# Expert routing by groups of tiles inside the second attention, and expert 0's and 1's weights split ahead

## Chip, cores and metric

One core of a Trainium2 chip. The metric is device microseconds (us) of one execution. Engines: TensorE (PE, weight loads PEld), VectorE (DVE), ScalarE (ACT), GpSimd (POOL); SyncE (SP) only issues transfers.

## The reference, cut to what matters

x is 8 sequences of 512 rows of 512 values, which is 4096 tokens; two layers follow each other:

```
x = x + xattn0(layernorm(x), ctx, mask)      # 16 heads of 32, 77 keys
x = x + ffn0(layernorm(x))                   # 8-bit x, ternary w, depthwise conv, silu
x = x + xattn1(layernorm(x), ctx)            # 16 heads of 64
x = x + moe(layernorm(x))
# moe: logits = x @ router (8 experts); the two best; softmax over the two
#      for each expert e over its tokens: out += w * ((silu(x@w13[e][:, :1024]) * (x@w13[e][:, 1024:])) @ w2[e])
```

## The kernel before, in words

The program is a chain of blocks; all engines meet between two of them: `context`, `attention0`, `ffn`, `attention1`, `routing`, `experts`, `combine` (`program`, L2083 on). A tile is 128 tokens, so there are 32 (NT), four to a sequence (TPS). x stays in SBUF. Products that need more than bf16 are made of a high and a low bf16 part, three products in place of one (PRODUCTS).

**attention0** runs a software pipeline of 35 steps. In step s PE does the scores of tile s (`score_half`, twice), the mix of tile s-2, the turn of tile s+1, the output product of tile s-3 and four flips of tile s-1. Both halves of the scores begin with two bf16 products that write the mask's bias into PSUM (L423); the score products add to it. DVE takes the maximum over PSUM (`shift`, L552), subtracts it into the SBUF buffer `e` (L556), sums after ACT's exponential (L565) and inverts; POOL multiplies by the inverse (L397) and adds the output bias (L400). PE may overwrite a half's scores once DVE has subtracted. Turns, flips and mixes share a ring of three PSUM banks in the fixed order of `unit`. At tile 8, POOL also issues one transfer (L392) that fills all of `sorted_x` in DRAM with zeros: 9216 rows of 2 KB.

**ffn** runs nine iterations over the sequences. In each, POOL multiplies 16 chunks (L1124, after ACT's row of scales L1336) and adds 16 (L1135); ACT's silu and rounding wait for POOL chunk by chunk, through four buffers. DVE is the busiest engine.

**attention1** is the same sort of pipeline. In every four steps, two turn two tiles of the next sequence each (`turns`) and two project the next sequence's queries (`projections`, 48 products of 512 columns each step). Units of the three-bank ring are freed by ACT's copy (`unit_copied`) or by DVE's low part (`unit_low`); `place` fixes their order. The output product of a tile is 24 products (L790). SP loads keys and values per sequence.

**routing** normalizes all 32 tiles (DVE L1677), turns them (PE L1605), and makes logits for groups of four tiles with the router as the stationary operand (L1585, then turned back, L1594). DVE then takes one chain of small operations over all tiles at once (L1685 to L1749): the two best experts, counts, a prefix sum over tiles, a region of `sorted_x` for each expert that begins where the last one's ends, rounded up to 128 rows, and the row of every token in it. Only then each tile is normalized again (L1755), split into high and low (ACT L1657, DVE L1763) and scattered by two indirect DMAs on POOL's queue (L1567). Between these tiles ACT and DVE split the weights of experts 0 and 1, 24 chunks of 128x1024 (L1636, L1669), into `plan.weights13` and `plan.weights2`.

**experts** goes over 72 slots of 128 rows (SLOTS, L1467); each does the products of one expert, whose number PE reads from `plan.expert`. SP loads slot rows from `sorted_x` (L1897, L1902) and stores results to `sorted_y`. POOL splits the weights of experts 2 to 7 as places come free (L1881, L1883). **combine** gathers two rows for each token from `sorted_y` (L2058) and adds them to x.

Of the kernel before, what the change touches and what calls it, by code (L numbers as in the profile page):

```python
# [27 lines left out]
P = 128  # L28
B, S, D = 8, 512, 512
KEYS = 77  # L30
H = 16
# [282 lines left out]
def attention0(nc, core, keys, values, w):  # L314
# [6 lines left out]
    FILL_AT = 8  # L321
    with ExitStack() as stack:
# [15 lines left out]
        zero_row = sb("zero_row", [P, 2 * D], BF16)  # L338
# [8 lines left out]
        scores_ready = sem("scores_ready"); topped = sem("topped"); shifted = sem("shifted")  # L347
# [3 lines left out]
        row_zeroed = sem("row_zeroed"); cleared = sem("cleared")  # L351
        block = stack.enter_context(nc.Block("attention0"))

# [30 lines left out]

        @block.gpsimd
        def _(pool):
            nc.gpsimd.memset(zero_row[:, :], 0.0).then_inc(row_zeroed, 1)
            pool.wait_ge(bo_in, 16)
            for t in range(NT):
                if t == FILL_AT:  # L390
                    pool.wait_ge(row_zeroed, 1)
                    pool.dma_start(w["sorted_x"].rearrange("(s p) d -> p s d", p=P),  # L392
                                   zero_row[:, :].unsqueeze(1).broadcast_to([P, SLOTS, 2 * D])).then_inc(cleared, 16)
# [7 lines left out]
            pool.wait_ge(cleared, 16)  # L401

        @block.tensor
        def _(pe):
# [13 lines left out]
            def score_half(t, half):  # L418
                b = t // TPS
                if t >= 1:  # L420
                    pe.wait_ge(shifted, 2 * (t - 1) + half + 1)
                for g in range(2):
                    nc.tensor.matmul(scores[half][:, g, 0:QUARTER], core.ident_bf[:, :],  # L423
                                     bias[:, t, :].unsqueeze(1).broadcast_to([P, CH, KEYS]), start=True, stop=False)
                for c in range(CH):
                    for g in range(2):
# [3 lines left out]
                                                start=False, stop=(c == CH - 1))  # L430
# [32 lines left out]
            for step in range(NT + 3):  # L463
                if step < NT:
                    pe.wait_ge(unit_copied, unit["turn", step] + 1)
                    pe.wait_ge(bias_made, step // TPS + 1)
                    for half in range(2):
                        score_half(step, half)
# [13 lines left out]
        def _(act):  # L482
# [42 lines left out]
            for step in range(NT + 2):  # L525
# [10 lines left out]
                if 1 <= step <= NT:  # L536
                    for q in range(ROWS_OF):
                        flipped(step - 1, q)

        @block.vector  # L540
        def _(dve):
# [6 lines left out]
            def shift(t, half):  # L548
                raw = scores[half][:, :, 0:QUARTER].rearrange("p g (h k) -> p g h k", h=CH)
                tops = top[:, half, :].rearrange("p (g h) -> p g h", g=2)  # L550
                dve.wait_ge(scores_ready, 2 * t + half + 1)
                nc.vector.tensor_reduce(tops, raw, AX.X, ALU.max).then_inc(topped, 1)  # L552
                dve.wait_ge(topped, 2 * t + half + 1)
                if t >= 2:
                    dve.wait_ge(unit_ready, unit["flip", t - 2, 2 * half + 1] + 1)
                nc.vector.tensor_tensor(grouped(e[:, t % 2, half, :]), raw,  # L556
                                        tops.unsqueeze(3).broadcast_to([P, 2, CH, KEYS]), ALU.subtract
                                        ).then_inc(shifted, 1)
# [33 lines left out]
def attention1(nc, core, w):  # L592
# [7 lines left out]
    WIDTH = PER * KEYS  # L600
    with ExitStack() as stack:
# [5 lines left out]
        xn_t = sb("xn_t", [P, 2, KD, S], BF16)  # L607
        query = [sb(f"query{i}", [P, 2, CH, S], BF16) for i in range(2)]
        keys = sb("keys", [P, 2, 2, CH, KEYS], BF16)
        values = sb("values", [KEYS, 2, CH * P])  # L610
# [3 lines left out]
        probs_t = sb("probs_t", [P, 2, H, P])  # L614
        mixed_t = sb("mixed_t", [P, 2, 2, CH, P], BF16)
        wq = sb("wq", [P, 2, KD, CH * P], BF16)
        wo = sb("wo", [P, 2, CH, D], BF16)
        bq = sb("bq", [P, CH])


        raw_q = probs_t[:, :, :, :].rearrange("p t h n -> p (t h n)").rearrange("p (k n) -> p k n", k=KD)
        raw_o = query[1][:, :, :, :].rearrange("p a c n -> p (a c n)").bitcast(F32).rearrange(
            "p (k n) -> p k n", n=D)
# [15 lines left out]
        out_ready = sem("out_ready"); out_added = sem("out_added"); stats_made = sem("stats_made")  # L639
# [831 lines left out]
def routing(nc, core, plan, w, sorted_x):  # L1471

    E = EXPERTS
# [669 lines left out]
```

## Time and profile before

| | |
|---|---|
| three runs | 3048.58, 3050.35, 3052.56 us; median 3050.35 |
| profiled execution, its own time | 3052.12 us |
| its span in the trace | 3050.3 us |
| granted PE clock, mean | 0.919 |
| PE busy | 2499.0 us, 82% |

A line of the timeline has start and length in us, engine, line of the kernel, operation, result and operands, how many, and in brackets the idle time of the engine before it with what ended it. A group's line ends with busy us, mean ns of one, and idle us before. Busy time excludes waits, except that an operation held up after it began shows as a longer one.

### The profile page before, as it was taken

The numbers are of one execution on the slowest core, as the hardware profiler recorded it, in microseconds if no ns is written. First come the engines' busy times: TensorE is split into PE (matmuls) and PEld (weight loads), VectorE is DVE, ScalarE is ACT, GpSimd is POOL, SyncE is SP. The second block draws the span as 40 slices with busy tenths as digits, with TensorE's granted clock in tenths as the row PEclk, the third lists the DMA queues.
The fourth block names the chain that finished last, engine by engine and source line by source line (L and its number), as shares of the span: only waits on it lengthen the run. The fifth ranks groups of instructions, "written<-read, shape, count | busy, mean of one in ns | idle before, by whom it ended". The sixth has DMA issues, their size and how long they took to land. (4 is left out here: it accounts for less than half of the span.)

```text
span 3050.3 us, 46845 instructions
## 1 busy us (share of the span) xinstructions
PE 2499.0 (82%) x16388; PEld 1340.7 (44%) x16603; DVE 1610.2 (53%) x2256; ACT 1083.4 (36%) x1736; POOL 971.9 (32%) x803
## 2 busy tenths in 40 slices
PE   8899964566656699999980299999999999999960
PEld 5566632222222355565640144444444444444430
DVE  4566668899897556566656322232333323332225
ACT  2355535788876444444342211111111111111110
POOL 0243312677768111111105400050643406320027
PEclk9799986798988799999995699999999999999985
DMA  6350010000000200000035301030322303220128
GB/s 229 116 214 36 2 56 0 1 1 1 0 1 0 72 10 14 10 14 10 1 97 171 143 28 34 28 117 28 117 82 77 100 30 114 72 62 28 34 74 274
DMA packets 88750, 190.29 MB, mean 62 GB/s; under 512 B 25189, under 2 KB 28261, under 8 KB 88117
## 3 DMA queue, kind: packets, MB, share of 16 engines
q1 hardware_dynamic: 63269, 98.43, 9.9%
q0 software_dynamic: 25360, 90.21, 8.9%
q8 instruction: 81, 1.33, 0.2%
q14 instruction: 40, 0.33, 0.0%
HBM read 120.65 MB, written 67.96 MB: 62 GB/s over the span
## 5 line engine op out<-in xcount | busy, mean ns | idle before, releaser
L1926 PE MATMUL e_gate_up<-weights,e_x_t 128*128 x3314 | 758.0, 380 | 9.2 <-ACT e_x_t L1980 1.8
L1926 PEld LDWEIGHTS e_gate_up<-weights,e_x_t 128*128 128x128 bf16 x3456 | 332.7, 98 | 376.9 <-issue 4.3
L2013 DVE TENSOR_TENSOR e_mid<-e_gate,e_gate_up 128x512 f32<-128x512 f32 x144 | 99.1, 688 | 644.7 <-ACT e_gate L1986 644.7
L1946 PE MATMUL e_out<-weights,e_mid_t 128*128 x1726 | 384.6, 379 | 1.2 <-DVE e_mid_t L2026 1.1
L1986 ACT ACTIVATE e_gate<-e_gate_up 128x512 f32<-128x512 f32 x144 | 86.1, 598 | 682.4 <-PE e_gate_up L1926 682.4
L1946 PEld LDWEIGHTS e_out<-weights,e_mid_t 128*128 128x128 bf16 x1728 | 169.1, 98 | 204.8 <-issue 1.2
L1205 PE MATMUL f_out<-f_w,hidden 128*128 128x512 f16 x512 | 141.3, 402 | 102.6 <-ACT hidden L1307 101.9
L708 POOL TENSOR_TENSOR a_e<-a_e,a_total 128x616 f32<-128x616 f32 x64 | 76.5, 1217 | 452.4 <-DVE a_total L960 452.4
L1135 POOL TENSOR_TENSOR f_shared<-f_shared 128x512 f32<-128x512 f32 x128 | 181.2, 1416 | 122.4 <-DVE f_shared L1413 122.4
L1876 POOL TENSOR_TENSOR e_token<-e_token 1x1 f32<-1x1 f32 x6 | 1.1, 184 | 657.5 <-PE e_out L1946 657.5
L1124 POOL TENSOR_TENSOR hidden<-hidden,f_up_row 128x512 f32<-128x512 f32 x128 | 178.6, 1406 | 86.6 <-ACT f_up_row L1336 86.6
L2026 DVE COPY e_mid_t<-e_mid_flip 128x1024 bf16<-128x1024 bf16 x144 | 98.9, 688 | 181.7 <-PE e_mid_flip L1936 181.7
L736 PE MATMUL a_ring<-a_xn_t,a_wq 128*128 128x512 bf16 x752 | 169.1, 382 | 7.8 <-issue 7.0
L790 PE MATMUL a_out<-a_wo,a_mixed_t 128*128 128x512 bf16 x737 | 164.3, 379 | 4.5 <-issue 3.0
L1184 PE MATMUL f_product<-f_xq_t,f_w 128*128 128x512 bf16 x489 | 140.0, 413 | 30.3 <-DVE f_padded L1381 18.5
L1992 ACT ACTIVATE e_y_rows<-e_out 128x512 f32<-128x512 f32 x72 | 43.0, 597 | 340.2 <-PE e_out L1946 340.2
L1413 DVE SCALAR_TENSOR_TENSOR f_shared<-f_padded,f_conv_w,f_shared 128x512 f32<-128x512 f32 x128 | 152.1, 1189 | 14.6 <-ACT f_shared L1290 14.3
L2058 POOL DMA_INDIRECT o_y<-sorted_y,plan_rows x64 | 68.8, 1075 | 284.6 <-PEq L2044 265.4
L1883 POOL TENSOR_TENSOR weights<-raw_weights,weights 128x1024 bf16<-128x1024 f32 x72 | 154.0, 2140 | 6.1
L397 POOL TENSOR_TENSOR a_e<-a_e,a_total 128x616 f32<-128x616 f32 x64 | 76.5, 1217 | 196.1 <-DVE a_total L567 196.1
L1916 PE MATMUL e_flip<-ident_bf,e_x_rows 128*128 128x128 bf16 x576 | 44.3, 220 | 114.5 <-DMA e_x_rows<-sorted_x 114.5
L2019 DVE TENSOR_TENSOR e_mid_parts<-e_mid,e_mid_parts 128x512 bf16<-128x512 f32 x144 | 130.3, 905 | 5.0
(236 smaller groups left out, 4134.0 us busy)
## 6 DMA issues: line engine op xcount, KB each, us to landing
raw_weights<-in_w POOLq DMA_DIRECT2D x72, 512.0 KB, 3.9
sorted_x<-a_zero_row POOLq DMA_DIRECT2D x1, 18432.0 KB, 57.0
e_x_rows<-sorted_x SPq DMA_DIRECT2D x72, 256.0 KB, 2.7
sorted_y<-e_y_rows SPq DMA_DIRECT2D x72, 256.0 KB, 2.0
raw_weights<-in_w SPq DMA_DIRECT2D x24, 512.0 KB, 3.7
x<-in_x SPq DMA_DIRECT2D x4, 2048.0 KB, 20.1
out<-x SPq DMA_DIRECT2D x32, 256.0 KB
hidden<-in_w_t SPq DMA_DIRECT2D x1, 4096.0 KB, 17.4
```

Source lines behind the costliest of these rows:

```text
L736: last = nc.tensor.matmul(bank(u)[:, :], wq[:, a, k, c * P:(c + 1) * P], xn_t[:, d, k, :], start=(k == 0 and a == d == 0), stop=(k == KD - ...
L790: last = nc.tensor.matmul(out[:, :], mixed_t[:, t % 2, a, c, :], wo[:, d, c, :], start=(c == 0 and a == d == 0), stop=(c == CH - 1 and (a, ...
L1124: nc.gpsimd.tensor_tensor(hidden[:, j, :], hidden[:, j, :], up2_row[:, :], ALU.mult).then_inc(scaled_up, 1)
L1135: nc.gpsimd.tensor_tensor(y[:, j % BUF, :], y[:, j % BUF, :], side[:, j % BUF, :], ALU.add).then_inc(right_added, 1)
L1184: last = nc.tensor.matmul(product[j % 2][:, :], w1[:, k, j % HC * P:(j % HC + 1) * P], xq_t[:, parity, k, :], start=(k == 0), stop=(k == K ...
L1205: last = nc.tensor.matmul(out[i][:, :], hq[:, j, i * P:(i + 1) * P], w2[:, j, :], start=False, stop=(j == HC - 1))
L1413: nc.vector.scalar_tensor_tensor(y[:, j % BUF, :], padded[:, j % BUF, 0:S], conv_w[:, j, 0:1], y[:, j % BUF, :], ALU.mult, ALU.add).then_i ...
L1883: nc.gpsimd.tensor_tensor(parts[1], plan.raw[:, n % 2, :], parts[0], ALU.subtract).then_inc(split, 1)
L1926: last = nc.tensor.matmul(gate_up[half][:, part, :], x_t[:, u, a, k, :], plan.weights13[:, bass.ds(expert % 2, 1), b, k, col:col + 512], s ...
L1946: last = nc.tensor.matmul(out[:, :], mid_t[:, a, j, :], plan.weights2[:, bass.ds(expert % 2, 1), b, j, :], start=(j == 0 and a == b == 0), ...
L2013: nc.vector.tensor_tensor(mid[:, half, :], gate[:, half, :], gate_up[half][:, 1, :], ALU.mult).then_inc(mid_made, 1)
L2019: nc.vector.tensor_tensor(mid_parts[:, half, 1, :], mid[:, half, :], mid_parts[:, half, 0, :], ALU.subtract).then_inc(mid_low, 1)
```

## The change

1. **Routing moves into attention1**, in nine groups of tiles: seven of four, then two of two. A group's small statistics (`moments`, `norms`; an ACT square root between exponentials), the logits (`logits_of`, tokens as the stationary operand, 8 columns), the choice (`choose`) and the rows (`counts`, `rows_of`) take places at fixed steps behind the tiles: pairs are turned again at the group's last tile + 5 and + 6, the choice and the rows follow one and two steps on. The pipeline has 39 steps in place of 35. The units `route`, `logits` and `counts` join the three-bank ring.
2. **Each expert gets a region of 4096 rows** of `sorted_x` (33792 rows with a margin), so that a group's rows are known without the counts of later tiles. POOL splits (`split`) and scatters (`scatter`) group by group. `slots_and_weights`, once at the end, works out which slot starts where (`plan.base`) and the rows in `sorted_y` (`plan.y_rows`). SP reads a slot's start from SBUF before its load.
3. **The zero fill moves** from attention0 to ffn's iteration 1, ahead of POOL's wait there, and is four transfers of 8448 rows.
4. **Experts 0 and 1**: their 24 chunks are loaded and split in attention0 (steps 4 to 27, high part on ACT, low part on POOL), stored to DRAM as bf16, and loaded in attention1 by SP: expert 0 during its last steps, w13 of expert 1 after the last output product, w2 of expert 1 after the last scatter has landed.
5. **The mask in attention0** is added by DVE while it moves the scores from PSUM into `e`; maximum and subtraction then work in SBUF. The bias products on PE go. PE may overwrite a half's scores after that addition.
6. **71 slots** in place of 72.
7. attention1's large buffers are laid over the expert weights' places.

```diff
-                for g in range(2):
-                    nc.tensor.matmul(scores[half][:, g, 0:QUARTER], core.ident_bf[:, :],
-                                     bias[:, t, :].unsqueeze(1).broadcast_to([P, CH, KEYS]), start=True, stop=False)
...
+                nc.vector.tensor_tensor(grouped(now), raw, bias[:, t, :].unsqueeze(1).unsqueeze(1).broadcast_to(
+                    [P, 2, CH, KEYS]), ALU.add).then_inc(biased, 1)
+                nc.vector.tensor_reduce(top[:, half, :], heads(now), AX.X, ALU.max).then_inc(topped, 1)
+                nc.vector.tensor_tensor(heads(now), heads(now), top[:, half, :].unsqueeze(2).broadcast_to(
+                    [P, HALF, KEYS]), ALU.subtract).then_inc(shifted, 1)
...
+                n = t - SPLIT_AT                        # POOL, attention0
+                if 0 <= n < len(early):
+                    pool.wait_ge(high_made, n + 1)
+                    nc.gpsimd.tensor_tensor(parts[:, n % 2, 1, :], raw[:, n % 2, :], parts[:, n % 2, 0, :],
+                                            ALU.subtract).then_inc(low_made, 1)
...
+                if isinstance(b, int) and b == 1:       # POOL, ffn
+                    blocks = ROWS // P // FILLS
+                    for f in range(FILLS):
+                        part = w["sorted_x"][f * blocks * P:(f + 1) * blocks * P, :]
+                        pool.dma_start(part.rearrange("(s p) d -> p s d", p=P),
+                                       zero_row[:, :].unsqueeze(1).broadcast_to([P, blocks, 2 * D])
+                                       ).then_inc(w["cleared"], 16)
                 if has_back:
                     pool.wait_ge(row2_copied, b)
...
+            def logits_of(t):
+                for i in range(2):
+                    for k in range(KD):
+                        last = nc.tensor.matmul(bank(u)[:, i * E:(i + 1) * E], row_t[:, i, k, :], router[:, k, :],
+                                                start=(k == 0), stop=(k == KD - 1))
...
+                for t in route_turns(step):             # POOL, attention1
+                    split(t)
+                if step in rows_at:
+                    g = rows_at[step]
+                    pool.wait_ge(rows_made, g + 1)
+                    for t in GROUPS[g]:
+                        scatter(t)
...
+            sp.wait_ge(out_ready, NT)                   # SP, attention1
+            for a in range(2):
+                sp.dma_start(plan.weights13[:, 1, a, :, :], w["split13"][1, a].rearrange("(k p) n -> p k n", p=P)
+                             ).then_inc(plan.early_in[1], 16)
+            sp.wait_ge(late_out, 32 * SENT)
+            for a in range(2):
+                sp.dma_start(plan.weights2[:, 1, a, :, :], w["split2"][1, a].rearrange("(k p) n -> p k n", p=P)
+                             ).then_inc(plan.early_in[1], 16)
...
+SLOTS = (2 * B * S) // P + EXPERTS - 1
+REGION = B * S
+FILLS = 4
+ROWS = EXPERTS * REGION + 1024
```

## Rows read from the trace of the kernel before

**Rows 1.** The page's head: the span

```profile
span 3050.3 us, 46845 instructions
```

**Rows 2.** Busy time of each engine by stage: stretch, length, PE, PEld, DVE, ACT, POOL

```profile
core 0: us, PE busy (x) PEld busy (x) DVE busy (x) ACT busy (x) POOL busy (x), PEclk, DMA share, GB/s
98.00:435.00 337.00, 320.35 (x3072) 221.28 (x3072) 213.52 (x348) 165.64 (x293) 119.88 (x105) 0.95 0.22 80
435.00:1003.00 568.00, 324.38 (x1341) 137.75 (x1364) 490.53 (x476) 398.70 (x626) 353.27 (x256) 0.83 0.02 7
1003.00:1547.00 544.00, 508.58 (x4689) 307.56 (x4736) 318.90 (x500) 236.37 (x395) 76.54 (x64) 0.97 0.07 18
1547.00:1730.00 183.00, 52.44 (x232) 25.04 (x233) 99.80 (x193) 66.40 (x100) 73.62 (x73) 0.65 0.48 164
1730.00:2951.00 1221.00, 1210.18 (x6767) 604.14 (x6908) 396.53 (x576) 197.45 (x289) 275.19 (x226) 1.00 0.19 61
```

**Rows 3.** Timeline of the routing stage: its two ends

```profile
1546.98 0.69 DVE L964 TENSOR_TENSOR x<-x,a_out 128x512 f32<-128x512 f32 x1 [4.79 <-PE a_out L790]
...
1718.46 0.97 POOL L1567 DMA_INDIRECT sorted_x<-r_xn_t,plan_rows  x1 [0.30 <-issue]
...
1727.01 0.82 SPq L1897 DMA_DIRECT2D e_x_rows<-sorted_x  x2
...
1729.66 1.04 PE L1916 MATMUL e_flip<-ident_bf,e_x_rows 128*128 128x128 bf16 x8 [114.47 <-DMA e_x_rows<-sorted_x]
```

**Rows 4.** Timeline of attention0: one step of a tile

```profile
250.18 0.80 DVE L552 TENSOR_REDUCE a_top<-a_scores 128x8 f32<-128x616 f32 x1 [1.68 <-PE a_scores L428]
...
258.27 0.43 PE L423 MATMUL a_scores<-a_bias,ident_bf 128*128 128x308 bf16 x2
...
258.63 1.12 PE L428 MATMUL a_scores<-keys,a_xn_t 32*128 32x77 f32 x16
...
259.79 0.80 DVE L552 TENSOR_REDUCE a_top<-a_scores 128x8 f32<-128x616 f32 x1 [1.68 <-PE a_scores L428]
```

**Rows 5.** Groups by line: what attention0 runs, and the weight splitting

```profile
L556 DVE TENSOR_TENSOR a_e<-a_scores,a_top 128x616 f32<-128x616 f32 x64 | 51.2, 800 | 2.2
...
L565 DVE TENSOR_REDUCE a_total<-a_e 128x8 f32<-128x616 f32 x64 | 50.7, 792 | 16.8 <-ACT a_e L502 15.1
...
L397 POOL TENSOR_TENSOR a_e<-a_e,a_total 128x616 f32<-128x616 f32 x64 | 76.5, 1217 | 196.1 <-DVE a_total L567 196.1
...
L400 POOL TENSOR_TENSOR x<-x,a_bo 128x512 f32<-128x512 f32 x32 | 40.7, 1271 | 0.0
...
L1636 ACT ACTIVATE weights<-raw_weights 128x1024 bf16<-128x1024 f32 x24 | 25.1, 1045 | 0.8 <-DMA raw_weights<-in_w 0.8
...
L1883 POOL TENSOR_TENSOR weights<-raw_weights,weights 128x1024 bf16<-128x1024 f32 x72 | 154.0, 2140 | 6.1
```

**Rows 6.** Tile e_mid_parts: least, median and longest ns of one subtraction

```profile
L2019 DVE TENSOR_TENSOR e_mid_parts<-e_mid,e_mid_parts x144: 691/693/2501, 1741.4 to 2939.9; 128x512 bf16<-128x512 f32 x144
```

**Rows 7.** Timeline of PE: two tiles turned; four logits tiles turned back

```profile
1230.39 1.34 PE L725 MATMUL a_ring<-ident,a_xn 128*128 128x128 f32 x8
...
1567.22 0.41 PE L1594 MATMUL r_logits_p<-ident,r_prefix 8*128 8x8 f32 x4
```

**Rows 8.** Groups by line, 1607:1626: one small DVE operation of routing

```profile
L1698 DVE TENSOR_TENSOR r_gap<-r_best 128x32 f32<-128x32 f32 x1 | 0.2, 192 | 0.0
```

**Rows 9.** Timeline of POOL: issue of the clearing transfer; idle before iteration 1

```profile
181.61 3.12 POOL L392 DMA_DIRECT2D sorted_x<-a_zero_row  x1
...
547.99 1.28 POOL L1124 TENSOR_TENSOR hidden<-hidden,f_up_row 128x512 f32<-128x512 f32 x1 [10.76 <-ACT f_up_row L1336]
```

**Rows 10.** DMA issues: KB each, us from issue to landing

```profile
sorted_x<-a_zero_row POOLq DMA_DIRECT2D x1, 18432.0 KB, 57.0
...
e_x_rows<-sorted_x SPq DMA_DIRECT2D x72, 256.0 KB, 2.7
...
a_probs_t<-in_wq_t SPq DMA_DIRECT2D x1, 2048.0 KB, 8.3
```

More of the change, by code:

```diff
@@ new lines, in attention1 @@
+        row_t = sb("row_t", [P, 2, KD, P])
+        sent = sb("sent", [P, SENT, 2, D], BF16)
+        before = sb("before", [P, P])
+        ones = sb("ones", [P, P])
+        order = sb("order", [P, E])
+        order_i = sb("order_i", [P, E], I32)
+        first_i = sb("first_i", [P, E], I32)
+        slot_i = sb("slot_i", [P, SLOTS], I32)
+        slot_f = sb("slot_f", [P, SLOTS])
+        norm_tmp = sb("norm_tmp2", [P, 5, TPS])
+        logits = sb("logits", [P, TPS, E])
+        mark = sb("mark", [P, TPS, E])
@@ new lines, in attention1 @@
+        rank = sb("rank", [P, TPS])
+        chosen = sb("chosen", [P, 2, TPS, E])
+        both = sb("both", [P, TPS, E])
+        run = sb("run", [P, TPS + 1, E])
+        upto = sb("upto", [P, E])
+        rows = sb("rows", [P, 2, NT])
+        best = sb("best", [P, 2, NT])
+        gap = sb("gap", [P, NT])
+        slots_of = sb("slots_of", [P, E])
+        ends = sb("ends", [P, 2, E])
+        slot_e = sb("slot_e", [1, 2, SLOTS])
+        first_f = sb("first_f", [P, E])
+        jump = sb("jump", [P, E])
@@ L711, in _ @@
+            for i in range(SENT):
+                pool.wait_ge(sent_out[i], 32 * LATE // SENT)
+            pool.wait_ge(late_out, 32 * SENT)
         @block.tensor
@@ L784, in output @@
             def output(t):
-                pe.wait_ge(unit_low, low[unit["mix", t, 1]] + 1)
+                pe.wait_ge(unit_low, low[unit["mix", t, 1]])
                 if t >= 1:
@@ L799, in _ @@
                 project(0, c)
-            for step in range(NT + 3):
+            for step in range(STEPS):
                 if step < NT:
@@ L815, in _ @@
                         flip(step - 1, q)
+                for t in route_turns(step):
+                    turn(("route", t))
                 for c in projections(step):
@@ L890, in _ @@
                                          ).then_inc(weights_high, 1)
-            norm(TPS)
-            norm(TPS + 1)
-            for step in range(NT + 2):
-                if step >= 2:
+            norm(("turn", TPS))
+            norm(("turn", TPS + 1))
+            for step in range(STEPS):
+                if 2 <= step < NT + 2:
                     mixed(step - 2, 0)
```

748 lines of the change are left out of this document (387 added, 361 removed).

## The prediction

> **What bounds the kernel now.** The forecast is against the profiled execution, 3052.1 us (span 3050.3, about 1.8 around it [rows 1]); the median of the three runs shown is 1.7 lower. I read the windows by stage first, then the timeline at the seams, then groups and DMA issues. By stage, PE is busy 320 of 337 us in attention0, 509 of 544 in attention1 and 1210 of 1221 in experts: these three are PE's, at the full granted clock but for their first microseconds. ffn is DVE's (491 of 568), with POOL at 353 in series with it. The routing stage is nobody's: in 183 us PE does 52, DVE 100 [rows 2]. The timeline shows its length as a reader should measure it: the last output product is in at 1546.98 (DVE's addition starts), the first slot's turn starts at 1729.66, PE idle 114.5 us before it, and before that POOL issues the last scatter at 1718.46 and SP the first slot load at 1727.01 [rows 3]. So 182.7 us lie between the products of attention1 and those of experts.
>
> **1. That gap.** Nearly all of it goes, but a tail stays for the tiles that are late by nature. Counted from the last output product: addition, statistics and `moments` some 2.7 us; a small DVE operation takes 0.19 us [rows 8], 0.21 with its semaphore. `logits_copy` and 12 operations of `rows_of` for tiles 24 to 27 end at about 6.6; choice (13) and `norms` (6) for the last pairs at 10.4; turn, copy, logits, a second choice and the last rows at 21.5. POOL is behind that: from 6.6 on it has 8 scatters at 0.97 + 0.30 = 1.27 us [rows 3], two splits of 1.7 (half of 1.05 and 2.14, the 1024-column price [rows 5]), then 4 and 4 scatters: 6.6 + 10.2 + 3.4 + 5.1 + 5.1 = 30.4. The last scatter before was followed by 7.6 us until the block was over [rows 3]: 38. Then comes an ordering cost: SP issues w2 of expert 1, 2 MB, when the scatters have landed, and the first slot's rows stand behind it in the same queue: 8.3 us as a 2 MB load [rows 10], then 2.7 [rows 10]: about 49. `slots_and_weights` (some 35 small operations, 10 us) runs beside the scatters. So 182.7 - 49.5 = **-133**; bounds -148 (no queueing, quicker landing) and -118 (cold PE, slower transfers).
>
> **2. PE in attention1.** PE is the bound there, so what it gets is paid. Two tiles' turns take 1.34 us: 0.67 each [rows 7]. Logits are four products per tile that stream only 8 columns; between four small ones with 8 rows of weights, 0.41, and a few with cold clock, 1.1 [rows 7], I take the turns' 0.67, since both load four full 128x128 fp32 weights. 28 tiles x 1.34 = 37.5 (the last four are in the tail). Counts: 7 x 0.5 = 3.5. A stall: where a logits unit follows two turns, the ring's bank is freed by DVE's low part of the second mix, which comes after the second `shift`, about 1.5 us after PE wants it, in 5 groups: 7.5. **+48**; bounds +32 and +65. The two table loads per group on ACT, the 25 to 30 small operations on DVE and POOL's splits and scatters I cost at nothing: ACT is busy 236 of 544, DVE 319, POOL 77 [rows 2], and the pipeline is two steps deep; without that cover they would be 9 x 2.6, 9 x 6 and 9 x 10 us.
>
> **3. 71 slots.** 1221 / 72 [rows 2]: **-17**, PE-bound, no doubt in it.
>
> **4. attention0.** A step takes 259.79 - 250.18 = 9.61 us with PE full; each bias pair delays the scores by 258.63 - 258.27 = 0.36 [rows 4], so PE would need 8.9. But DVE's shift grows from two passes to three of 0.80 [rows 5] per half, near 8.5 a step. And there is a collision. The new subtraction has both operands in SBUF; where POOL works on SBUF, such a subtraction took 0.69 at best and 2.50 at worst [rows 6], that is, it waited for POOL's 2.14 to end [rows 5]. POOL's order is multiply, multiply, bias, low part: from the end of the second subtraction it is 1.1 + 2 x 1.22 + 1.27 = 4.75 us until the low part starts [rows 5] (ACT's high part, 1.05 after its flips, is done at 4.65), and it holds to 6.9. The next tile's first subtraction is due at 5.3: it waits 1.6, and the loop through exponential, flip copies and scores closes at about 10.05. 24 steps x (10.05 - 9.61) = +10.6, the 8 without splitting x -0.7 = -5.6: **+5**; bounds -22 (no collision) and +20. DMA for the 24 chunks (0.5 MB in, 0.5 out per step) is hidden.
>
> **5. The zero fill in ffn.** Before, one fill of 9216 rows cost POOL 3.12 us to issue [rows 9], 57.0 to land [rows 10]. Now POOL issues four of 8448 rows at 2.9, in a place where it sat idle 10.76 us [rows 9]. If the queue takes them all, that is 11.5 against 10.8: +1, the lower bound. But what is issued has to be held somewhere until it has been moved, and no row of the trace shows more than those 9216 rows in flight; this asks for 33792 within 12 us, while one fill takes 57 to land. The upper bound is that each fill must wait until the one before has landed, 57.0 x 8448 / 9216 = 52.3: POOL is free again after 3 x 52.3 + 2.9 = 160 us, 149 later than before. What is queued behind it is `scale_up` and the addition of every chunk, and with four buffers everything in ffn waits after four chunks; some 6 us of DVE's work is done meanwhile. **+143**. Two full fills together (16896 rows) are 1.8 times the most that was seen in flight; I take the upper bound, since the only row of this kind is for a fill that had the queue to itself.
>
> The Trainium skill bears on this: "SBUF — State Buffer" (section "SBUF size: 192, 224, or 256?") sets aside 16 KiB a partition for POOL's descriptors, and "DMA: Bandwidth & Descriptors" (sections "Terms" and "SWDGE vs HWDGE vs iDMA") gives a descriptor 16 bytes and each direction 16 partitions. My estimate from these is 16384 rows in flight: two fills don't fit, by little. By that page alone the sum would be the upper bound if room is given back a whole transfer at a time. No row here shows a queue that is full.
>
> **Sum.** -133 + 48 - 17 + 5 + 143 = **+46**: 3052 + 46 = **3098 us**. combine and the rest of ffn are unchanged.
>
> **Rivals.**
> A. *The queue takes all four fills* (other side: faster). Place: POOL's queue at ffn's second iteration; it decides from the second fill on. For it: 9216 rows were taken in 3.1 us without a sign of waiting; against it: 3.7 times as much is asked for. -133 + 48 - 17 + 5 + 1 = -96: 2956, 2925 to 2990. Chance 0.25.
> B. *Room is given back row by row.* POOL then writes as fast as rows land: 33792 rows take 4 x 52.3 = 209 us; POOL is free when the last 9216 (57) are left, or with room for nearly twice as many, about 110: 152 to 110, less 10.8 and 6: +93 to +135. 3048 to 3090. Chance 0.13.
> C. *Fill by fill, as forecast.* 0.62; within it the collision in attention0 fails to happen in a third of cases, which gives 3072. Its own range is 3068 to 3125.
> That the change doesn't do what it says (fewer slots, less work between the stages) I see no way for.
>
> **How the numbers follow.** About 0.2% (6 us) can be told from no change. Slower: C but for 0.02, and most of B (0.07) = 0.67; faster: A, 0.02 of B and a remnant of C = 0.29; same 0.04. The likeliest is 3098. Range 2955 to 3125: C with its bounds, B, and the upper half of A; left out are the lower half of A (0.12) and C's edges. Cases of both signs hold weight, so C's own range above is the one to read if POOL's stall is there.
>
> **What would show it.** In the profile after: POOL idle or long issues at ffn's second iteration with about 52 us between fills, PE's granted clock at its low level there, and ffn some 140 us longer; if the four issues stand within 12 us, step 5 is wrong and A holds. attention0: the first half's subtraction with a mean of 2 us or more in steps 4 to 27 and steps of 10 us; steps of 8.9 would refute it. attention1: about 48 us longer to its last product, with turns and logits of 0.67 a tile; then 45 to 55 us to the first turn of experts, with the slot's load landing 10 us or more after its issue. A slot remains 17.0. If the gap is above 65 us, POOL's scatters were slower than 1.27; if attention1 grows by over 70, the ring or DVE, not PE's own work, bounds it.

## The result and the profile after

The changed kernel takes 3150.77 us (median of 4 runs, 3148.74 to 3156.01) against 3049.47: a ratio of 1.0335, 95% interval 1.0317 to 1.0353. Slower, as forecast, but by 101 us where 46 were forecast, and 26 us above the end of the range. The profiled execution spans 3154.2 us, 103.9 more than the one of before.

By stage, the windows of the kernel after (columns as in [rows 2]; the rows are attention0, ffn, attention1 to its last product, the gap, experts):

```profile
core 0: us, PE busy (x) PEld busy (x) DVE busy (x) ACT busy (x) POOL busy (x), PEclk, DMA share, GB/s
98.10:440.90 342.80, 305.71 (x2944) 211.88 (x2944) 278.73 (x405) 191.14 (x316) 166.82 (x121) 0.89 0.29 95
440.90:1162.30 721.40, 328.78 (x1341) 139.13 (x1364) 495.48 (x490) 400.53 (x629) 364.38 (x270) 0.76 0.28 102
1162.30:1803.50 641.20, 584.63 (x5050) 364.39 (x5099) 372.70 (x777) 290.01 (x474) 175.24 (x177) 0.92 0.14 45
1803.50:1845.00 41.50, 10.90 (x60) 9.84 (x58) 21.92 (x101) 5.51 (x9) 20.62 (x25) 0.55 0.70 260
1845.00:3055.00 1210.00, 1198.53 (x6674) 592.99 (x6816) 392.80 (x568) 195.82 (x284) 276.43 (x226) 1.00 0.19 62
```

| stage, us | before | after | difference | forecast |
|---|---|---|---|---|
| context | 96.6 | 98.1 | +1.5 | 0 |
| attention0 | 334.7 | 342.9 | +8.1 | +5 |
| ffn | 571.9 | 721.3 | +149.4 | +143 |
| attention1, to the last addition | 543.8 | 641.3 | +97.5 | +48 |
| gap, to the first turn of experts | 182.7 | 41.5 | -141.2 | -133 |
| experts | 1220.9 | 1210.0 | -10.9 | -17 |
| combine | 99.7 | 99.2 | -0.5 | 0 |

One term is off by more than 9 us: attention1, by 49.5 of the 58 that are missing. PE is busy 585 us there where it was 509, and the granted clock is 0.92 where it was 0.97 [rows 2]. At two levels of 1.0 and 0.5 (2.4 and 1.2 GHz), a mean of 0.92 means, as an estimate, 16% of 641 us, or 103 us, at the low level; before it was 6% of 544, or 33.

**ffn.** The timeline of POOL after, at ffn's iteration 1, answers to [rows 9]:

```profile
547.30 2.92 POOL L1487 DMA_DIRECT2D sorted_x<-f_zero_row  x1
598.48 2.85 POOL L1487 DMA_DIRECT2D sorted_x<-f_zero_row  x1 [48.26 <-issue]
649.55 2.82 POOL L1487 DMA_DIRECT2D sorted_x<-f_zero_row  x1 [48.22 <-issue]
700.58 2.83 POOL L1487 DMA_DIRECT2D sorted_x<-f_zero_row  x1 [48.20 <-issue]
703.43 3.71 POOL L1480 TENSOR_TENSOR hidden<-hidden,f_up_row 128x512 f32<-128x512 f32 x3
```

The four issues stand 51 us apart, each 2.9 us long, and POOL starts its first multiplication 156 us after the first issue, at 703.43. Before, it was idle for 10.8 us at this point.

**The gap.** The timeline from attention1's last addition to the first turn, which answers to [rows 3]:

```profile
1803.52 0.69 DVE L1187 TENSOR_TENSOR x<-x,a_out 128x512 f32<-128x512 f32 x1 [1.22 <-PE a_out L979]
...
1832.93 0.96 POOL L852 DMA_INDIRECT sorted_x<-weights,plan_rows  x1 [0.30 <-issue]
...
1835.62 0.98 SPq L821 DMA_DIRECT2D weights<-split  x2
...
1841.41 0.09 POOL L1926 MEMSET e_token<- 1x3 f32 x1 [7.53 <-POOLq L634]
...
1842.39 1.54 SPq L1978 DMA_DIRECT2D e_x_rows<-sorted_x  x2
...
1845.04 1.04 PE L1997 MATMUL e_flip<-ident_bf,e_x_rows 128*128 128x128 bf16 x8 [18.69 <-DMA e_x_rows<-sorted_x]
```

POOL's last scatter ends at 1833.9, 30.4 us after the addition began: the chain of 16 scatters and two splits came out to the tenth of a us in all. POOL is then held for 7.5 us as before, and 3.6 us later PE has its rows. w2 of expert 1 was issued at 1835.62, inside those 7.5 us.

**attention1.** The groups of PE's products in attention1 (a pair's logits are 8 products, which the trace shows as 16 records; before, all turns took 22.8 us, a pair of them 1.34 us [rows 7]; the last line is the output product in the kernel before):

```profile
L979 PE MATMUL a_out<-weights 128*128 128x512 bf16 x736 | 184.2, 412 | 4.4 <-issue 2.9 <-DVE weights L1161 0.3 <-DVE a_logits L1222 0.2
...
L891 PE MATMUL a_ring<-ident,a_xn 128*128 128x128 f32 x247 | 41.5, 309 | 17.3 <-ACT a_xn L1031 13.1 <-DVE weights L1161 3.7
...
L903 PE MATMUL a_ring<-a_router,a_row_t 128*128 128x8 f32 x224 | 32.5, 282 | 8.3 <-DVE weights L1161 7.5 <-ACT a_row_t L1039 0.7
```

```profile
L790 PE MATMUL a_out<-a_wo,a_mixed_t 128*128 128x512 bf16 x737 | 164.3, 379 | 4.5 <-issue 3.0 <-DVE x L964 0.9
```

The logits are 32.5 us, the turns 41.5, and the output product of 24 full-width matmuls, which the change leaves alone, takes 412 ns a record where it took 379, which adds some 20 us (184.2 against 164.3). What goes with it stands in the timeline of two steps (the first three lines, then the last three) and the windows beside the second:

```profile
1340.51 0.63 PE L891 MATMUL a_ring<-ident,a_xn 128*128 128x128 f32 x4 [1.25 <-DVE weights L1161]
1342.64 2.71 PE L903 MATMUL a_ring<-a_router,a_row_t 128*128 128x8 f32 x16 [1.51 <-DVE weights L1161]
1345.58 7.52 PE L979 MATMUL a_out<-weights 128*128 128x512 bf16 x23 [0.23 <-issue]
...
1356.80 1.97 PE L967 MATMUL a_ring<-weights,raw_weights 77*64 77x128 f32 x32
1358.70 1.95 PE L903 MATMUL a_ring<-a_router,a_row_t 128*128 128x8 f32 x16
1360.78 6.75 PE L979 MATMUL a_out<-weights 128*128 128x512 bf16 x23
```

```profile
1356.00:1360.00 4.00, 4.00 (x92) 3.77 (x86) 2.99 (x4) 2.27 (x5) 0.00 (x0) 1.00 0.01 4
1360.00:1364.00 4.00, 3.87 (x14) 1.82 (x15) 3.82 (x10) 0.72 (x1) 1.58 (x2) 0.58 0.00 0
```

At the full clock the logits take 1.95 us a pair, not 1.34. In the second step PE is idle for no more than 0.13 us before or after them, and yet the granted clock goes from 1.00 to 0.58 in the next 4 us: the output product takes 6.75 us where 5.13 is its length at the full clock. In the first step PE had waited 1.25 us ahead of the last turns and 1.51 us ahead of the logits, and the clock is at 0.50 from 1344 to 1350 (windows of 2 us); there the output product takes 7.52.

### The profile page after: what moved, and what is told of

Same layout as the page of the kernel before. It is cut to its first block and busy times, and to the rows that moved or that the text cites. A ratio compares the mean times of both kernels' runs of the same rounds, so it can differ in the third digit from the quotient of the medians.

```text
span 3154.2 us, 47443 instructions
## 1 busy us (share of the span) xinstructions
PE 2512.8 (80%) x16357; PEld 1363.7 (43%) x16571; DVE 1651.6 (52%) x2498; ACT 1101.0 (35%) x1744; POOL 1074.8 (34%) x895
## 5 line engine op out<-in xcount | busy, mean ns | idle before, releaser
L2007 PE MATMUL e_gate_up<-weights,e_x_t 128*128 x3268 | 748.0, 380 | 9.0 <-ACT e_x_t L2061 1.8
L2107 DVE COPY e_mid_t<-e_mid_flip 128x1024 bf16<-128x1024 bf16 x142 | 97.5, 687 | 180.9 <-PE e_mid_flip L2017 180.9
L1568 PEld LDWEIGHTS f_out<-f_w,hidden 128*128 128x128 f16 x512 | 42.7, 102 | 335.8 <-ACT hidden L1670 298.4
L979 PE MATMUL a_out<-weights 128*128 128x512 bf16 x736 | 184.2, 412 | 4.4 <-issue 2.9
L1744 DVE TENSOR_TENSOR f_padded<-f_product,f_down_row 128x512 f32<-128x512 f32 x128 | 87.6, 684 | 183.8 <-PE f_product L1547 176.0
L925 PE MATMUL a_ring<-weights 128*128 128x512 bf16 x752 | 169.5, 383 | 8.1 <-issue 7.3
L2139 POOL DMA_INDIRECT o_y<-sorted_y,plan_y_rows x64 | 67.7, 1058 | 268.6 <-PEq L2125 249.4
## 6 DMA issues: line engine op xcount, KB each, us to landing
sorted_x<-f_zero_row POOLq DMA_DIRECT2D x4, 16896.0 KB, 50.8
```

The costliest lines, as they stand in the source:

```text
L925: last = nc.tensor.matmul(bank(u)[:, :], wq[:, a, k, c * P:(c + 1) * P], xn_t[:, d, k, :], start=(k == 0 and a == d == 0), stop=(k == KD - ...
L979: last = nc.tensor.matmul(out[:, :], mixed_t[:, t % 2, a, c, :], wo[:, d, c, :], start=(c == 0 and a == d == 0), stop=(c == CH - 1 and (a, ...
L1568: last = nc.tensor.matmul(out[i][:, :], hq[:, j, i * P:(i + 1) * P], w2[:, j, :], start=False, stop=(j == HC - 1))
L2007: last = nc.tensor.matmul(gate_up[half][:, part, :], x_t[:, u, a, k, :], plan.weights13[:, bass.ds(expert % 2, 1), b, k, col:col + 512], s ...
L2139: pool.indirect_dma_start(out=y[:, t % BUFFERS, c, :], out_offset=None, in_=sorted_y, in_offset=bass.IndirectOffsetOnAxis(ap=plan.y_rows[: ...
```

## The experiments

### Where POOL's 150 us went: spread and eighths

`spread` issues the four fills in four iterations of ffn:

```diff
-                if isinstance(b, int) and b == 1:
+                fills = {0: (0,), 1: (1,), B - 2: (2,), B - 1: (3,)}
+                if isinstance(b, int) and b in fills:
                     blocks = ROWS // P // FILLS
-                    for f in range(FILLS):
+                    if b == 0:
+                        pool.wait_ge(w2_in, 16)
+                    for f in fills[b]:
```

> The changed kernel with its four fills issued in four different iterations of ffn (0, 1, 6, 7; the one in iteration 0 once ffn's second weights have landed) in place of all four in iteration 1. Theory: a fill of 8448 rows is taken by the queue at once when the one before has landed (51 us), so no issue waits; ffn falls from 721 to about 572 us and the kernel from 3151 to 3002 us (3000 to 3010). Rival (the fills cost ffn time by what they move, not by where POOL waits): each still costs some 20 us or more, 3030 to 3100 us.

Measured: 3010.35 us (3005.69 to 3012.63), 0.9853 of before (0.9835 to 0.9872). ffn takes 578.1 us in place of 721.3, 6 more than before. The fills move the same bytes; nearly all that they cost was POOL's wait. With this one edit the changed kernel takes 1.5% less than before, a small difference, but its interval leaves no change out.

`eighths` sets `FILLS = 8` with all eight at iteration 1.

> The changed kernel with eight fills of 4224 rows in place of four of 8448, all still at ffn's iteration 1. A fill of 4224 rows should land in 25.5 us. If the queue takes only one transfer at a time whatever its size, POOL waits for seven: 179 us, 3176 us. If it waits for room by rows and gives it back a transfer at a time, two in flight (8448 rows) give 153 us as now (3151 us) and three in flight (12672 rows) give 128 us: 3125 us.

Measured: one run of 3145.07 us, ffn 717.0. The timeline of POOL's issues in eighths (x3 are three issues one behind another):

```profile
543.47 5.55 POOL L1487 DMA_DIRECT2D sorted_x<-f_zero_row  x3
617.32 5.44 POOL L1487 DMA_DIRECT2D sorted_x<-f_zero_row  x3 [68.31 <-issue]
691.05 3.62 POOL L1487 DMA_DIRECT2D sorted_x<-f_zero_row  x2 [68.30 <-issue]
```

The times from issue to landing of the eight:

```profile
DMA to landing us min/median/max: 26.9/48.4/69.8
```

None of the three mechanisms came, although the time lies 6 us from the second number. Three fills, 12672 rows, were taken at once, so more than 8448 rows fit; but the fourth was not taken when the first had landed (the shortest landing is 26.9 us after its issue). It was taken 68 us after the third had been issued, when all three had landed (the longest landing is 69.8 us after its issue), and the seventh likewise after the next three. So POOL's queue, once an issue doesn't fit, waited until it was empty. That gives 3 + 3 + 2 and nearly the same wait as four single fills, 151 us from the first issue to the first multiplication against 156. The Trainium skill, "DMA: Bandwidth & Descriptors" (sections "Terms" and "SWDGE vs HWDGE vs iDMA") with "SBUF — State Buffer" (section "SBUF size: 192, 224, or 256?"), led to my estimate of 16384 rows in flight: the run agrees, as 12672 were taken and 16896 not.

### Why attention1 grew twice as much as forecast: wide, onek, behind, late

All four are edits of `spread`, whose attention1 takes 642.5 us:

```profile
1016.70:1659.20 642.50, 592.04 (x5099) 366.83 (x5100) 373.18 (x778) 290.30 (x474) 175.59 (x177) 0.91 0.14 45
```

`wide` streams 128 columns in each logits product and reads 8 of them:

```diff
-                        last = nc.tensor.matmul(bank(u)[:, i * E:(i + 1) * E], row_t[:, i, k, :], router[:, k, :],
+                        last = nc.tensor.matmul(bank(u)[:, i * 128:(i + 1) * 128], row_t[:, i, k, :],
+                                                router[:, k, :].unsqueeze(1).broadcast_to([P, 16, E]),
...
```

> The spread kernel with the logits products of attention1 streaming 128 columns (the router's 8 columns 16 times over) in place of 8; same number of products and weight loads, same logits. Theory T (the granted clock falls in and after the logits because PE streams almost nothing while it loads weights; this costs about 35 of the 97 us by which attention1 grew): the clock stays at 1.00 after the logits, the outputs behind them go back from 6.4 or 7.5 to 5.1 us, and the kernel is 20 to 35 us faster than spread, though 16 products of 128 columns take up to 0.3 us more a pair. Rival (the clock falls because PE stands idle at the ring's bank): no gain, or 4 us slower.

Measured: 2993.99 us (2989.30 to 2999.79), 0.980 of before; attention1 629.1 us, its granted clock 0.93 against 0.91. The output product behind one pair's logits, in spread and then in wide; both times PE had waited 1.51 us just before the logits:

```profile
1357.47 8.14 PE L979 MATMUL a_out<-weights 128*128 128x512 bf16 x24
```

```profile
1356.08 5.34 PE L980 MATMUL a_out<-weights 128*128 128x512 bf16 x24
```

So what theory T said of this place came: with 128 columns the clock stayed up behind most of the logits. The gain that it named (20 to 35 us) did not; the windows below say where the rest went.

`onek` keeps 2 of a pair's 8 logits products (k = 0 of each tile).

> The spread kernel with 2 of the 16 logits products per pair; it leaves out three quarters of the router's product and one accumulation, so the choice of experts is another one. It removes 14 products of 0.122 us at 14 of 16 pairs' places inside attention1: 24 us of PE by their price at full clock. Theory T: the clock's loss goes too, 45 to 60 us faster than spread in attention1. Rival (the clock has another cause): 24 us. The experts stage may differ a little, so attention1's own length is to be read.

(In this text 16 stands for the records of a pair; the kernel keeps 2 of 8 products.)

Measured: 2984.10 us (2980.89 to 2985.62); attention1 614.5 us, 28 less than spread. The three quarters of the 34.7 us that spread spends on logits are 26. So the removed work is nearly all of the gain (PE's busy time is 26.3 us less), and the clock stayed at 0.92. The 45 to 60 us of theory T did not come.

`behind` moves the logits and counts on PE behind the output product; nothing is removed:

```diff
-                if step - 1 in pairs_at:
-                    logits_of(pairs_at[step - 1])
-                if step in rows_at:
-                    counts(rows_at[step])
                 if step == 3:
                     pe.wait_ge(weights_low, 2 * KD)
                 if 3 <= step < NT + 3:
                     output(step - 3)
+                if step - 1 in pairs_at:
+                    logits_of(pairs_at[step - 1])
+                if step in rows_at:
+                    counts(rows_at[step])
```

> The spread kernel with PE doing the logits and the counts of a step behind that step's output product in place of ahead of it; the order of the ring's banks stays. Theory S (DVE's low parts of the mixes hold the ring's banks, 7.6 us of waits ahead of the logits, and small products back to back, mixes, turns and logits, bring the granted clock down): the waits ahead of the logits go (-7.6) and the output product of 23 full-width matmuls parts the small work, so that time at the low clock goes down from 112 us towards 50: attention1 15 to 35 us shorter. Rival (the clock answers to the total of small work in a stretch, whatever its order): -8 us, from the waits alone. Rival 2: DVE, which copies the logits ahead of its next work, now waits 5 us for them and hands it on: 0 or slower.

Measured: 2971.03 us (2969.95 to 2972.04), 0.9733 of before (0.9717 to 0.9749), 39 us faster than spread. Attention1's window and its groups:

```profile
1017.30:1619.90 602.60, 553.41 (x5067) 350.17 (x5115) 366.58 (x777) 291.69 (x476) 175.50 (x177) 0.97 0.15 50
```

```profile
1197.11 5.13 PE L979 MATMUL a_out<-weights 128*128 128x512 bf16 x23
1202.07 1.85 PE L903 MATMUL a_ring<-a_router,a_row_t 128*128 128x8 f32 x16
...
1209.81 5.13 PE L979 MATMUL a_out<-weights 128*128 128x512 bf16 x23 [0.16 <-issue]
```

```profile
L979 PE MATMUL a_out<-weights 128*128 128x512 bf16 x736 | 164.2, 379 | 4.9 <-issue 3.0 <-DVE x L1187 1.2
...
L891 PE MATMUL a_ring<-ident,a_xn 128*128 128x128 f32 x248 | 39.5, 295 | 19.8 <-ACT a_xn L1031 13.1 <-DVE weights L1161 6.3
...
L903 PE MATMUL a_ring<-a_router,a_row_t 128*128 128x8 f32 x235 | 27.3, 251 | 0.7 <-ACT a_row_t L1039 0.7
```

Attention1 is 39.9 us shorter than in spread, a little above the 15 to 35 that theory S named. PE's busy time is 38.7 us less, and its idle time (602.6 - 553.4 = 49.2, against 642.5 - 592.0 = 50.5) is the same within 1.3 (behind's trace lacks 32 of the 768 records of the output product and shows 3 us idle at them, spread's lacks none and shows 0, so the waits may have given up to 4 us of the gain): the waits ahead of the logits went, but others came at the turns and, behind the counts, at the flips. So the gain is in the main not the waits, as the first rival had it, but the clock: 0.97 in place of 0.91 is 36 us at the low level in place of 116, and 80 us at half speed are 40 us of lost work. The output product is back at 379 ns a record.

How the order does it is less plain than theory S had it. Logits stand in two steps of a group. In the first of them in the changed kernel, 12.7 us pass between two output products (1332.84 to 1345.58), waits of 1.25 and 1.51 us among them; in behind 8.4 us pass there (1188.75 to 1197.11). In the second step it is 7.8 us in the one and 7.7 in the other, with the same products in another order, and yet the next output product took 6.75 us in the changed kernel and 5.13 in behind.

`late` puts one memset on DVE ahead of attention1 in spread and changes nothing in its steps:

> The spread kernel with one memset of 2464 columns (some 2.6 us) on DVE at the start of attention1; nothing else in attention1 is changed. If the time lost to the low clock depends on how the steps fall against the chip's own rhythm, attention1 differs from spread's 642.5 by more than the 2.6 us put in (the same code took 619.9 to 642.5 in five kernels that reach it at different times), its time at the low clock differing from 112 us with it. If it depends on the code alone, 645.

Measured: one run of 2988.01 us. Its attention1 takes 618.4 us:

```profile
1017.30:1635.80 618.50, 571.22 (x5050) 356.26 (x5099) 373.79 (x779) 289.26 (x473) 174.75 (x172) 0.94 0.14 46
```

That is 24 us less than spread; the memset, 2.1 us long, stands ahead of this window. The whole kernel, by one run, takes 22 us less. PE's granted clock is 0.94. The same steps took 641.3 in the changed kernel, 642.5 in spread, 638.0 in eighths, 624.9 and 619.9 in mask_rows and nolow below. So attention1's time varies by up to 24 us among kernels whose steps are the same and that begin it at other times (one trace each), and the totals of `wide` and `onek` can't be judged against spread alone: 13 us of difference lie inside this band, and 28 are little more. A part of the band is a wait: PE waits for DVE ahead of its scores for 13.6 to 13.9 us in all in the changed kernel, spread and eighths, for 8.2 to 8.3 in the other three. With the logits behind the output product attention1 took 602.6, 602.5 and 602.7 us in three kernels (behind, quarters, lag), and 605.9 in `best`, which also had the wide logits: there the width brings nothing. Against the shortest stage in the old order the new order is 16 us shorter, against spread 40.

The place of the low clock tells more than its total. Windows of 1 us over attention1 give, as us at the low level (rounded, one trace each) by what stands where the fall begins:

| | in all | first 90 us | logits or the output product behind them | PE's wait ahead of the scores | last 40 us |
|---|---|---|---|---|---|
| before | 30 | 30 | - | 0 | 0 |
| spread | 111 | 36 | 51 | 10 | 14 |
| late | 76 | 35 | 37 | 0 | 3 |
| wide | 82 | 38 | 14 | 24 | 7 |
| onek | 95 | 34 | 20 | 27 | 14 |
| behind | 37 | 37 | 0 | 0 | 0 |

In the six kernels with the old order and the full logits of 8 columns, 37 to 51 us stand at the logits. With 128 columns it is 14 and with a quarter of the products 20, so the logits' own shape and number have a part in it; but both kernels lost 24 and 27 us behind waits of up to 2.2 us ahead of the scores, where spread lost 10. Behind the output product the logits cost none.

### attention0 and the gap: nolow, mask_rows, quarters, lag

The changed kernel's subtraction in attention0, by tile (least, median and longest ns):

```profile
L586 DVE TENSOR_TENSOR a_e<-a_e,a_top x64: 799/801/2162, 108.2 to 418.6; 128x616 f32<-128x616 f32 x64
```

`nolow` cuts POOL's low part to 8 columns (with the low halves cleared once ahead of the stage).

> The spread kernel with POOL's 24 low parts in attention0 cut to 8 columns each; it leaves out the low parts of the weights of experts 0 and 1 (they are zero). Theory (collision: DVE's subtraction inside SBUF waits for POOL's low part, and this sets the step): the longest subtraction falls from 2.16 to under 1.3 us, the step from 10.3 to about 9.0 to 9.6 us, attention0 from 341 to 300 to 320 us. Rival (DVE's third pass or PE's clock sets the step): 335 to 341 us.

Measured: one run of 2949.62 us. The same subtraction:

```profile
L588 DVE TENSOR_TENSOR a_e<-a_e,a_top x64: 799/800/802, 107.6 to 377.0; 128x616 f32<-128x616 f32 x64
```

The group's 64 subtractions take 51.2 us, 0.80 each, where they took 77.0 in the changed kernel. Attention0 takes 302.1 us, 39 less than spread, and its clock is 0.95 against 0.89. The collision was there, and it cost more than the forecast's 24 steps of 1.15, or 28 us. (`nolow` also takes the low parts' time off POOL; `quarters` below keeps it there.)

`mask_rows` restores the bias products on PE with maximum and subtraction from PSUM, and moves w2 of expert 1 behind the first rows:

```diff
-            sp.wait_ge(late_out, 32 * SENT)
-            for a in range(2):
-                sp.dma_start(plan.weights2[:, 1, a, :, :], ...
...
                 sp.dma_start(x_rows[:, s, :], x_rows_of(s)).then_inc(x_in[s], 16)
+            for a in range(2):
+                sp.dma_start(plan.weights2[:, 1, a, :, :], ...
```

> The spread kernel with two independent edits, read from their own stages: the mask's bias goes back to PE and the maximum and subtraction back to PSUM in attention0, and w2 of expert 1 is loaded behind the first two slots' rows. Attention0: if the collision of the third pass sets the step, it falls from 10.3 to 9.6 us (PE-bound, the clock stays at 1.00) and the stage from 341 to 335; if POOL's low part alone lengthens POOL's own chain enough, it stays at 341. Gap: the first turn comes 8 us earlier (41.6 to 33.5), by the 8.3 us of a 2 MB load; if x's rows were not queued behind it, nothing changes.

Measured: 2983.01 us (2977.73 to 2985.75). Attention0 takes 331.8 us (337.3 with the same edit in best) against 341.2: putting the mask on DVE cost 4 to 9 us here (attention0 differs by 5.5 us between these two kernels though its instructions are the same), beside POOL's low parts; without them (nolow) it gains 33 over before. The gap is 42.3 us against 41.6, so the order of the loads brings nothing:

```profile
1662.74 0.96 POOL L848 DMA_INDIRECT sorted_x<-weights,plan_rows  x1 [0.30 <-issue]
...
1671.23 0.09 POOL L1925 MEMSET e_token<- 1x3 f32 x1 [7.52 <-POOLq L634]
...
1672.21 1.53 SPq L1977 DMA_DIRECT2D e_x_rows<-sorted_x  x2
1673.78 1.06 SPq L1979 DMA_DIRECT2D weights<-split  x2
...
1674.87 1.03 PE L1999 MATMUL e_flip<-ident_bf,e_x_rows 128*128 128x128 bf16 x8 [18.72 <-DMA e_x_rows<-sorted_x]
```

The rows are issued ahead of w2 and yet the first turn comes as late. What holds it is the end of POOL's block, 7.5 us after the last scatter; w2 had passed in its shadow.

`quarters` is `behind` with each low part as four subtractions of 256 columns:

```diff
-                    nc.gpsimd.tensor_tensor(parts[:, n % 2, 1, :], raw[:, n % 2, :], parts[:, n % 2, 0, :],
-                                            ALU.subtract).then_inc(low_made, 1)
+                    for q in range(4):
+                        cut = slice(q * CW // 4, (q + 1) * CW // 4)
+                        low = nc.gpsimd.tensor_tensor(parts[:, n % 2, 1, cut], raw[:, n % 2, cut],
+                                                      parts[:, n % 2, 0, cut], ALU.subtract)
+                    low.then_inc(low_made, 1)
```

> The behind kernel with each of POOL's 24 low parts in attention0 as four subtractions of 256 columns in place of one of 1024. Collision theory: DVE's subtraction inside SBUF waits only for the piece that runs (about 0.55 us), so its longest falls from 2.16 to about 1.3 us and attention0 goes from 342 to 308 to 318 us; the kernel from 2971 to about 2941. Rival (POOL keeps the port through back-to-back instructions of its own): the subtraction still takes 2.2 us or more, 342 us.

The two operations in one step of behind, and then of quarters:

```profile
243.39 2.13 POOL L423 TENSOR_TENSOR a_parts<-a_raw,a_parts 128x1024 bf16<-128x1024 f32 x1
...
244.03 2.15 DVE L586 TENSOR_TENSOR a_e<-a_e,a_top 128x616 f32<-128x616 f32 x1
```

```profile
248.15 3.12 POOL L425 TENSOR_TENSOR a_parts<-a_raw,a_parts 128x256 bf16<-128x256 f32 x4
...
249.01 1.09 DVE L589 TENSOR_TENSOR a_e<-a_e,a_top 128x616 f32<-128x616 f32 x1
```

In behind, POOL's low part begins 0.6 us ahead of DVE's subtraction, which ends 0.66 us after POOL's does. In quarters the same subtraction takes 1.09 us (the longest of all 64 is 1.34), and POOL's four pieces take 3.12 together. Attention0 takes 310.4 us, and the kernel 2940.72 (2938.20 to 2943.77), 0.9632 of before (0.9615 to 0.9648): the fastest version of this study, 3.7% below the kernel before and 6.7% below the changed one. The Trainium skill, "SBUF — State Buffer" (section "Who interferes with whom"), has DVE and GpSimd share a pair of ports as an exclusive lock for the length of an instruction; this agrees, 2.15 us with one long piece and 1.09 with short ones.

`lag` is `behind` with the low part of a chunk a step later and ahead of POOL's bias addition.

> The behind kernel with POOL's low part of a chunk done a step later and ahead of the bias addition in place of behind it, so that it runs from 242.2 to 244.3 where it ran from 243.4 to 245.5 and DVE's subtraction is due at 244.0 (times of the step read in behind's trace). Collision theory: the subtraction waits 0.3 us at most, attention0 comes near the 302 us of nolow: 302 to 315; the kernel 2971 - 30 to 40 = 2931 to 2941. Rival (the addition of the bias, one SBUF operand pair too, now falls on the subtraction and holds it as long): 330 to 342 us.

Measured: 2956.07 us (2953.51 to 2958.23), 15 less than behind; attention0 326.0 us.

```profile
241.26 2.14 POOL L421 TENSOR_TENSOR a_parts<-a_raw,a_parts 128x1024 bf16<-128x1024 f32 x1
...
243.37 1.26 POOL L424 TENSOR_TENSOR x<-x,a_bo 128x512 f32<-128x512 f32 x1
243.37 1.92 DVE L586 TENSOR_TENSOR a_e<-a_e,a_top 128x616 f32<-128x616 f32 x1
```

The low part is now over when the subtraction is due at 243.37, but the bias addition starts at the same moment, and the subtraction takes 1.92 us. The time lies between the two expectations, and the mechanism is the rival's: I had looked for a place free of the low part and not of POOL.

`best` joins spread, wide, behind and both edits of mask_rows.

> Spread, wide, behind, and the two edits of mask_rows together, same output as the reference's. By the sum of separate gains if they add: 3010 - 15 (wide) - 15 (behind) - 6 - 8 = 2966 us. If wide and behind act on the same loss of clock, 2975 to 2985. Rival: one undoes another and it stays at 2994 or above.

Measured: 2965.43 us (2960.95 to 2972.24), 0.9714 of before (0.9697 to 0.9730), close to the plain sum of 2966, but not by the parts named there: behind gave 39 and not 15, wide and the order of the rows nothing, and its interval and behind's overlap.

## Why the prediction was right and wrong, point by point

- **Fills (+143 forecast, +149 measured): right.** Case C, fill by fill, held: 51 us between issues, 2.9 us each, POOL late by some 145. Rival A, that the queue takes all four, is refuted by the trace, and B by the equal distances. The reason given, that each fill waits until the one before has landed, is only half of it: eighths shows that the queue waits until all in flight have landed.
- **Gap (-133 forecast, -141 measured): right, with one wrong term.** POOL's chain of 30.4 and the 7.6 behind it stood as forecast. The 8.3 us of w2 ahead of the rows were counted as a term of their own; they ran beside the 7.6, as mask_rows shows.
- **attention0 (+5 forecast, +8 measured): right in mechanism, and close by luck.** The collision of DVE's new subtraction with POOL's low part stood where the working had put it. But two sizes were off and nearly cancelled: without the collision the forecast had -22 and nolow shows -33; the collision was priced at 28 and cost some 40. PE, with time to spare, also ran at a lower clock (0.89 against 0.95), which the working did not have.
- **One slot (-17 forecast, -11 measured).** A slot went, but the other 71 turned slower by 0.08 us each:

```profile
L2061 ACT ACTIVATE e_x_t<-e_flip x71: 1018/1019/1023, 1846.1 to 3020.5; 128x1024 bf16<-128x1024 bf16 x71
```

(3020.5 - 1846.1) / 70 = 16.78 us between first and last turn, before (2916.1 - 1730.7) / 71 = 16.70. The base that SP now reads for each slot is a candidate; it wasn't tested.
- **PE in attention1 (+48 forecast, +97.5 measured): the step that failed.** It read "PE is the bound there, so what it gets is paid", and priced what PE gets by rows at the full clock. In behind, where the clock is as before (0.97), attention1 grew by 58.8 us: turns 16.7, logits 27.3, counts 4.1 and 2.5 for the rest, less 6 because the groups' times overlap, makes 44.8 of busy time; 14.0 are idle. The forecast was 37.5 + 3.5 = 41 of work and 7.5 of waits, so it was short by 10: 4 of work, since a pair's logits cost some 1.85 us and not the 1.34 of two turns (turns cost a little less than forecast), and 6.5 of idle time. The other 38.7 us, between behind and the changed kernel, were in the main no work: the same products took longer. The added turns and logits stood in one row with scores, mixes and turns, ahead of the output product, with short waits between, and the granted clock fell there again and again; behind the output product it didn't. That attention1 is PE's "at the full granted clock but for their first microseconds" was read from before, and nothing in the working asked what the new order would do to that clock. The sign that the prediction named for growth above 70 us, "the ring or DVE, not PE's own work, bounds it", points the wrong way for most of it: behind keeps the waits within 1 to 4 us and takes 39 us off. The 1.1 that the working names for logits at a cold clock is not among rows 7.
- No rival and no bound covered this: the upper bound of +65 was all work and waits. That is why the range ended at 3125.

What stays open: how the small products and the waits of up to 2.3 us share in bringing the clock down. wide and onek show that the logits' shape and number have a part at their place; late, that the total also moves with nothing changed in the steps. What is shown is that with the logits behind the output product the low clock at them is gone but for the stage's last 40 us (one fall each in quarters and `best`, near the last logits and counts), and that the old order's cost varied by 24 us; why the same length of small products costs the clock in one order and not in the other is not shown.

## What to carry to other kernels

A matmul-bound stage pays twice for small matmuls that are added to it: once for their own time, and again if the clock falls under the wide product that follows. Try them on the other side of that product, and read the granted clock by short windows, as well as PE's busy time, before and after; the stage's total alone varied by 24 us here. Bulk transfers from POOL's queue want to be issued so far apart that each finds room in the queue (in spread they stood 61 us apart or more, 8448 rows of 2 KB each), and work of POOL that meets two-operand SBUF work of DVE is better cut into short pieces.

## What the runs showed of the hardware

- POOL's queue took 3 fills of 4224 rows within 5.6 us and held the fourth until all three had landed, 68 us later; it took one fill of 8448 rows and held the second for 48 us, until the first had landed (50.8).
- The granted clock fell from 1.00 to 0.58 in a 4 us window with PE busy for 3.87 of them, just after 1.95 us of products of 8 columns that PE entered and left with a pause of 0.13 us at most. The Trainium skill, "TensorE: Matmul & The Clock Gate" (section "Part 1: The HAM clock gate (the "warmup" mystery)"), ties the low level to PE's idle time; here PE was not idle, so the measurement goes beyond the rule.
- With 128 columns in place of 8 in those products, the output product behind them took 5.34 us where it had taken 8.14, and the low clock at this place fell from 51 us of the stage to 14; at other places it rose.
- The same steps of attention1 took 618 to 643 us in six kernels that reached them at different times, with a granted clock between 0.91 and 0.94; in another order 602.5 to 602.7 in three.
- A subtraction of DVE with both operands in SBUF took 0.80 us alone, 2.15 beside a long operation of POOL, 1.09 beside pieces of a quarter of it, and 1.92 beside POOL's bias addition.
